# Attention scores: adding the mask on VectorE while the scores move to SBUF, instead of by identity-by-mask matrix products

## What is computed

```python
# stage 1, grouped attention: 16 query heads, 4 key/value heads, D = 32
scores = einsum('btkgd,bskd->bkgts', qg, k) * scale
scores = scores + tril(ones)          # 1 is added at and below the diagonal
out = softmax(scores) @ v ; out @ wo.T + bo

# stage 5, causal cross attention: 16 heads, D = 32
scores = where(causal, qh @ kh.T / sqrt(32), finfo.min)
out = softmax(scores) @ v ; out @ Wout.T
```

## Time and profile before

| | us |
|---|---|
| median of 3 runs | 2407.41 |
| lowest and highest | 2405.82, 2408.34 |
| the profiled execution, as timed | 2409.18 |
| its span in the trace | 2407.4 |
| PE busy, DVE busy, ACT busy in the span | 2076.0, 1195.6, 812.7 |
| stage 1 (gqa), first weights to last sum, about | 40 to 322 |
| stage 5 (causal), the same, about | 1450 to 1741 |

### The profile page before, as it was taken

How to read it: one execution, slowest core, us unless ns; L and a number is a source line. 1 busy time by engine, 2 the same in 40 slices (tenths; PEclk the granted TensorE clock), 3 DMA queues, 4 the chain that set the end, 5 groups by cost and what they waited for, 6 DMA issues and landing times. The chain is left out here.

```text
span 2407.4 us, 33874 instructions
## 1 busy us (share of the span) xinstructions
PE 2076.0 (86%) x12898; PEld 1690.9 (70%) x12898; DVE 1195.6 (50%) x2044; ACT 812.7 (34%) x2401; POOL 276.6 (11%) x285
## 2 busy tenths in 40 slices
PE   4999958889999969999699977899779998999970
PEld 3777746777777747777577765677567777999970
DVE  4466743344444446333434454667643324565546
ACT  1445613333333332221121103454422113565542
POOL 0111100000000018000201100000105000000016
PEclk9799968999999989999899997899969998999995
DMA  5011133000000012000420001000024103666635
GB/s 172 1 37 37 37 131 120 14 1 1 1 1 1 1 53 92 1 0 0 169 111 1 1 22 40 1 1 1 1 89 163 37 0 122 246 241 223 247 123 188
DMA packets 58717, 164.35 MB, mean 68 GB/s; under 512 B 5088, under 2 KB 22880, under 8 KB 54368
## 3 DMA queue, kind: packets, MB, share of 16 engines
q1 hardware_dynamic: 30944, 82.72, 10.0%
q0 software_dynamic: 8432, 68.03, 7.8%
q10 hardware_dynamic: 19216, 11.89, 1.8%
HBM read 125.93 MB, written 36.70 MB: 68 GB/s over the span
## 5 line engine op out<-in xcount | busy, mean ns | idle before, releaser
L100 PE MATMUL banks<-expert_xgh,weh 128*128 128x256 f32 (+1 forms) x552 | 158.4, 287 | 1.4 <-DVE expert_xgl L1687 1.4
L102 PE MATMUL banks<-expert_xgh,wel 128*128 128x256 f32 (+1 forms) x552 | 156.6, 284 | 0.0
L101 PE MATMUL banks<-expert_xgl,weh 128*128 128x256 f32 (+1 forms) x552 | 156.0, 283 | 0.0
L1165 PE MATMUL banks<-ternary_xth,ternary_wq 128*128 (+1 forms) x352 | 138.8, 394 | 1.4 <-DVE ternary_xtl L73 1.4
L1165 PE MATMUL banks<-ternary_xtl,ternary_wq 128*128 (+1 forms) x352 | 138.5, 393 | 0.0
L388 ACT ACTIVATE causal_pr<-banks,causal_nb 128x128 f32<-128x128 f32 x256 | 89.9, 377 | 78.5 <-DVE causal_nb L511 78.5
L388 ACT ACTIVATE gqa_pr<-banks,gqa_nb 128x128 f32<-128x128 f32 x256 | 89.9, 377 | 74.3 <-DVE gqa_nb L511 74.3
L878 DVE TENSOR_TENSOR latent_ctl<-banks,latent_cth 128x512 fp32r<-128x512 f32 x64 | 44.2, 691 | 140.2 <-ACT latent_cth L819 140.2
L100 PE MATMUL banks<-latent_vh,latent_cth 128*128 128x512 f32 x256 | 104.2, 407 | 10.1 <-DVE latent_ctl L878 10.1
L555 PE MATMUL banks<-ident,X 128*128 128x128 f32 x192 | 37.1, 359 | 85.5 <-DVE gqa_xgl L485 32.0
L100 PEld LDWEIGHTS banks<-expert_xgh,weh 128*128 128x128 f32 (+1 forms) x552 | 100.7, 182 | 3.7 <-DVE expert_xgl L1687 1.8
(11 more groups left out here) (415 smaller groups left out, 5841.3 us busy)
## 6 DMA issues: line engine op xcount, KB each, us to landing
x_slots<-decay_zeros SPq DMA_DIRECT2D x46, 256.0 KB, 2.7
expert_xin<-x_slots SPq DMA_DIRECT2D x23, 512.0 KB, 5.3
y_slots<-expert_ys SPq DMA_DIRECT2D x23, 512.0 KB, 3.7
gqa_tw<-in_ternary_w ACTq DMA_DIRECT2D x4, 2112.0 KB, 10.5
ternary_raw<-in_ternary_w SPq DMA_DIRECT2D x11, 768.0 KB, 4.2
latent_qt<-in_latent_fold SPq DMA_DIRECT2D x6, 864.0 KB, 4.5
latent_kt<-in_latent_fold SPq DMA_DIRECT2D x6, 864.0 KB, 4.6
weights_raw<-in_expert_experts SPq DMA_DIRECT2D x2, 2176.0 KB, 8.0
```

Of the source, the lines that this page charges most:

```text
L100: pe.matmul(out, wh, xh, start=first, stop=False, **kw)
L101: pe.matmul(out, wh, xl, start=False, stop=False, **kw)
L102: return pe.matmul(out, wl, xh, start=False, stop=last, **kw)
L1165: a = pe.matmul(dst[:, :], wq[:, j, m, c * P:(c + 1) * P], x[:, c, toks], start=c == 0 and n == 0, stop=c == C - 1 and n == 1)
```

## The change

The two mask products in front of each softmax unit's scores are gone, and each score product now starts its own columns. DVE adds the mask, broadcast over eight heads, while it moves the 1,024 columns of scores from the two banks to `pr`; it then takes the maximum from `pr`. ACT computes the exponentials in place, `pr` to `pr`. The wait for the transposes of unit u-2 moves from ACT to DVE; DVE waits for its own sum and for the exponentials of unit u-2 (which read `nb`) before the maximum; PE waits at S(u) for the sum of unit u-2 (`masked`) instead of its exponentials. The copies of the identity and the mask that ACT made for the products go too.

```diff
@@ constants (ACT)
-                if soft:
-                    act.activation(identr[:, :], S.ident[:, :], ACT.Copy).then_inc(const_hi, 1)
-                    act.activation(maskr[:, :], (S.tril if kind == "gqa" else S.causal)[:, :], ACT.Copy).then_inc(const_hi, 1)
@@ S on ACT
                     act.wait_ge(max_done, u + 1)
-                    if u >= 2:
-                        act.wait_ge(pt_full, u - 1)
                     for c in range(8):
-                        a = act.activation(pr[:, h, c, :], S.bank[2 * h + c // 4][:, (c % 4) * P:(c % 4 + 1) * P], ACT.Exp,
+                        a = act.activation(pr[:, h, c, :], pr[:, h, c, :], ACT.Exp,
@@ S on DVE
+                    mask8 = (S.tril if kind == "gqa" else S.causal)[:, :].unsqueeze(1).broadcast_to((P, 8, P))
                     dve.wait_ge(s_full, u + 1)
-                    dve.tensor_reduce(nb[:, h, :], unit_banks(h), AX, ALU.max, negate=True).then_inc(max_done, 1)
+                    if u >= 2:
+                        dve.wait_ge(pt_full, u - 1)
+                    dve.tensor_tensor(pr[:, h, :, :], unit_banks(h), mask8, ALU.add).then_inc(masked, 1)
+                    dve.wait_ge(masked, u + 1)
+                    if u >= 2:
+                        dve.wait_ge(exp_done, u - 1)
+                    dve.tensor_reduce(nb[:, h, :], pr[:, h, :, :], AX, ALU.max, negate=True).then_inc(max_done, 1)
@@ S on PE
-                    if u == 0 and soft:
-                        pe.wait_ge(const_hi, 2)
                     if u >= 2:
-                        pe.wait_ge(exp_done if soft else pt_done, u - 1)
-                    if soft:
-                        for x in range(2):
-                            pe.matmul(S.bank[2 * h + x], identr[:, :], maskr[:, :].unsqueeze(1).broadcast_to((P, 4, P)),
-                                      start=True, stop=False)
+                        pe.wait_ge(masked if soft else pt_done, u - 1)
...
-                            if soft:
-                                m = pe.matmul(dst, q, k, start=False, stop=j == 3)
-                            else:
-                                m = pe.matmul(dst, k, q, start=True, stop=True)
+                            a1, a2 = (q, k) if soft else (k, q)
+                            m = pe.matmul(dst, a1, a2, start=True, stop=True)
```

More of the change, by code:

```diff
@@ L177, in attention_phase @@
             rts, on = sb("rts", [P, DM]), sb("on", [P, 2, DM])
-            maskr, identr = sb("maskr", [P, P], F32R), sb("identr", [P, P], F32R)
         if kind == "causal":
@@ L209, in attention_phase @@
         pp_full, pp_hi, free_d, free_a = sem("pp_full"), sem("pp_hi"), sem("free_d"), sem("free_a")
-        s_full, max_done, exp_done = sem("s_full"), sem("max_done"), sem("exp_done")
+        s_full, masked, max_done, exp_done = sem("s_full"), sem("masked"), sem("max_done"), sem("exp_done")
         pt_full, pt_done, rec_done, spread_done = sem("pt_full"), sem("pt_done"), sem("rec_done"), sem("spread_done")
```

## The result

| | before | after |
|---|---|---|
| median, us | 2407.77 (4 runs, 2405.82 to 2408.34) | 2422.74 (4 runs, 2417.52 to 2424.34) |
| ratio, 95% interval | | 1.006 (1.0042 to 1.0077) |
| profiled execution: as timed, span | 2409.18, 2407.4 | 2424.34, 2422.2 |

The change makes the kernel 15 us slower, by the medians. The forecast was 2426 with 2409 to 2440 around it.

The account below looks back on a forecast made before the run. PE was taken to bound the middle, a ring of DVE, ACT and PE the tails. Terms without clock +8.6, tail clock +9.6 and slot 5's clock +0.9 made +19 on 2407.4: 2426 us, 8 in 10 within 2409 to 2440.

Parts of the forecast that it names:

- Middle: Stage 1, units 1 to 7, 9 to 15, 17 to 23 and the mask of 24: 0.65 us gained each, -14.3.
- DVE hidden in the middle: In a middle block DVE needs 12.3 us of PE's 13.85, so PE never waits for a DVE result.
- Prices: Per unit: mask sum 1.25 us, maximum from SBUF 1.22, exponentials from SBUF 0 to 0.34 more, taken as 0.17.
- rival (d): Not slower, by a cheap maximum from SBUF: 2397 us, or 2403 to 2407 with part of the clock lost; chance 0.13.
- Slots 5 to 7 of stage 5: Evacuations stand behind sum and maximum: slots lose 1.25, about 0.7 and 0.8 us, +2.8 a group, +8.4 in three.
- Turns: At units 0, 8, 16 the chain gains the sum and loses the masks: +4.3 us, plus 1.0 for exponentials.
- Tails: Last four blocks of both stages: a DVE and PE ring of 12.87 us, +2.08 per block, two tails +17.4.
- The clock: In the tails a 3.1 us PE pause before the odd unit's transposes lowers the clock: 6 x 1.6 = +9.6 us.
- (a): The forecast itself, rings longer and the clock lost in the tails: 2426 us, own range 2419 to 2433; chance 0.45.
- (b): Same longer rings in the tails, but the clock stays: 2416 us (2412 to 2419); chance 0.25.
- (c): The low clock lasts into the next scores and the middle slips: 2434 to 2445 us; chance 0.12.
- (e): DVE's work is hidden everywhere, 64 x 0.65 = -42 us: 2366 us; chance 0.03.

Follow-up runs that it names:

- the kernel with both masks: The changed kernel with PE's mask products put back in all units, so the mask is added twice: 2450.95 us, ratio 1.0183.
- the kernel with its clock kept: The changed kernel with twelve unread products filling PE's pause before the transposes of each odd unit from 25 on: 2413.57 us, ratio 1.0038.
- the second run: The changed kernel, unaltered, measured again beside three of the experiments: 2420.96 us, ratio 1.0064.

## Why the prediction was right

**Middle.** Right in kind and a little large. A block takes 14.01 and not 13.85: units that follow pv gain 0.66, units that follow rt 0.49. Before, the mask product could start 0.35 after rt does (156.74, the row here, to 157.09 in the earlier trace rows); now the scores start 0.52 to 0.53 after rt (151.73 to 152.25, above; 272.83 in the tail, where the loads show 0.17 of "issue"). The price of 0.65 was read from mask to scores, and it should have been read from rt to scores in both cases. Over 22 units, half of each kind, that makes the gain 12.7 and not 14.3.

```profile
156.74 0.60 PE L612 MATMUL banks<-ident,gqa_spread 128*128 128x128 f32 x4
```

**DVE hidden in the middle.** Right; the kernel with both masks keeps the units' distances of before to 0.01 us, and the one without a mask has those of the changed kernel.

**Prices.** The mask sum was taken at 1.25 and runs at 1.223 plus 0.03 of semaphore; a stride of zero costs nothing. The maximum from SBUF, 1.220 against my 1.22, refutes rival (d). The exponentials cost +0.35 for eight, the upper end of 0 to 0.34 and not the 0.17 that I took: reading the sums hides nothing of it. The prediction's estimate from the fixed cycles in the Trainium skill ("VectorE: DVE Perf Modes", the TRN2 errata) was 0.35, and the trace agrees.

**Slots 5 to 7 of stage 5.** Predicted +1.25, +0.7, +0.8; measured +0.93, +0.75, +0.44 (8.15, 8.33 and 5.68 against 7.22, 7.58 and 5.24), 2.1 a group and not 2.8. In the first group slot 5 takes 9.71: the clock fell in it (0.50 in the window below) and in the other two groups' slot 5 it didn't. So the clock behind the pause cost 1.6 once, where I had 0.3 three times, and the three groups come to 8.0 against 8.4 and 0.9. The k copy starts 3.93 after the scores, not 4.35. The sum with `X` starts 0.33 ahead of the scores (1591.26), where I had 0.15, and a stretch of 1.86 follows it and not 2.01, so the mask's sum starts 1.53 and not 1.86 after them; sum and maximum then take 2.40 and not 2.5. The wait that was named is there, 1.92 on PE's products (2.35 on the weight load), and moving the copy removes it.

```profile
1527.50:1530.50 3.00, 3.00 (x14) 2.29 (x12) 1.38 (x2) 1.67 (x10) 0.00 (x0) 0.50 0.02 5
```

**Turns.** The wait for the next group's transposes goes from 4.52 to 6.05. That is +1.53, which the sum's 1.26 and the exponentials' 0.35 account for to 0.1; less 0.65 for the masks it is +0.9, and I had +0.6 and 0.17. From the scores of units 0, 8 and 16 to the next unit's, the six turns of the two stages grew by 6.9 (3.0 and 3.9), where I had 5.3; they differ among themselves by more than 1 us with the clock behind the wait.

```profile
131.67 1.97 PE L556 MATMUL banks<-ident,X 128*128 128x128 f32 x8 [6.05 <-DVE gqa_xgl L479]
```

**Tails.** The ring is the right one, as 12.25 in the kernel with its clock kept shows, and 0.62 too long in my sum (12.87 for 12.25). Four DVE instructions that were priced with 0.03 of semaphore overlap instead, 0.11 to 0.12 each, and the stretch from the sum with `X` is 1.87 where the mask products and the scores had made it 2.01. What I didn't see is a second ring through ACT that is only 0.25 shorter. It didn't matter for the forecast, but it decides what half a change in the tail is worth. The transposes' wait was forecast at 3.1 and is 3.03. The whole tails, from the scores of unit 24 to the latent stage's transposes and to the last sum with `X`, grew by 14.7 and 12.3, and I had 13.7 each. That this comes out is luck: three periods give 8.9 and 8.4 where I had 11.0 with the clock, and entry and exit 5.8 and 3.8 where I had 2.7. In the grouped tail the clock also fell once before the first of the three periods, which I hadn't counted.

**The clock.** Forecast (a) over (b), and so it went: the clock fell in all six blocks. It costs 1.3 to 1.6 a block (0.7 to 1.2 in one tail of the second run), where I had 1.6. The kernel with its clock kept is 9.8 above the kernel before of its series, where rival (b) had 8.6.

**Total.** The two changed stages cost +19.0 against a sum of +19.1. That they agree so closely is luck, since my sum was under by 2.6 in stage 1 and over by 2.7 in stage 5. The median is 3 under the forecast; in the profiled execution the untouched middle ran 5.2 shorter and stage 6 1.0 longer, which no term of the sum foresaw. Of the other rivals, (c) did not come: nothing slipped in the middle, and the clock was back before the next scores (the scores at 286.58 take 1.16, as 277.92 did at full clock). (e) would have needed the tails hidden.

## What to carry to other kernels

An average of busy shares said that DVE had half its time free; it was free only where PE had work to fill with. Split such a move by stretch: take work off the bounding engine where it is the bound, and leave it there where it waits in a ring with the engine that would get the work. Here that turned +0.6% into -1.0%. Where engines form a ring, list the second longest one too, and read what a pause in it does to TensorE's clock.

## What the runs showed of the hardware

- DVE instructions without a wait between them overlap. After one of 1.22 us the next starts after 1.13 to 1.14, after one of 0.68 after 0.59. The Trainium skill ("VectorE: DVE Perf Modes", The DRAIN you can't avoid) says that the next operation doesn't start until the pipe is empty, and adds that one which is not held starts earlier; these traces show the second.
- A pause of 1.15 us on TensorE in front of eight transposes was followed by the low clock in three of six blocks, one of 3.03 in all six, and the same pause filled with products in none.
- Where TensorE's clock is low moves from kernel to kernel in stages that a change doesn't touch, and their length with it. From latent to the first causal maximum the eleven profiled executions other than before's have 1153.4 to 1163.4 us, before's 1158.4; the shortest have 114 to 119 us at the low clock and the longest 142. A total that moves by less than this 5 us either way says little of an edit, and the stages have to be compared. What puts the low clock in one place or another there stays open.
